# Loads of the next x issued by ScalarE instead of SyncE, layer 1's masked scores ahead of the last turning, its exponentials later in ScalarE's order, in a two-layer graph attention kernel

## The chip, the cores and the metric

The kernel runs on one core of a Trainium2 chip. A core has a matrix engine (TensorE, PE in the profile; its weight loads are PEld), VectorE (DVE), ScalarE (ACT), GpSimd (POOL) and SyncE (SP), which here only issues transfers. Each engine works through its own list in order, and they meet by semaphores. 16 DMA engines serve the transfers of all issuers. The metric is the device time of one execution in microseconds; the time before is a median of three runs.

## The reference

`x` is 128 graphs of 128 nodes with 512 features, `adj` a 128 x 128 matrix of each graph. Two attention layers follow each other:

```python
# layer 0, 8 heads of 64
Q, K, V = x @ W_q + b_q, x @ W_k + b_k, x @ W_v + b_v
scores = einsum('bihd,bjhd->bhij', Q, K) / sqrt(64)
scores = scores + (a[:, :, None] + c[:, None, :] + b_g + log(adj + 1e-9))[:, None]   # a, c: x @ halves of w_g
x = einsum('bhij,bjhd->bihd', softmax(scores), V).reshape(B, N, D) + x
# layer 1, one head of 512
q, k = x @ Wq + bq, x @ Wk + bk
scores = where(adj == 0, -1e18, einsum('bod,bid->boi', q, k) / sqrt(512))
attn = where(adj == 0, 0, softmax(scores))
x = x + einsum('boi,bie->boe', attn, x) @ Wc
out = (x - mean) * rsqrt(var + 1e-5) * gamma + beta
```

## The kernel before

**Tiling.** The graphs are done in 32 groups of four (`GG = 4`, `NG = 32`). A group has 4 x 128 = 512 columns, so x is held turned, as four chunks `d` of 128 features by 512 columns. For precision every large product is three matmuls: each operand is split into a high part (`x_hi`, rounded, on ScalarE, L778) and the rest (`x_lo`, on GpSimd, L1518), and `hi_lo_part` (L244 to L246) multiplies high by high, high by low, low by high.

**Staging.** Iteration `t` of `step` does layer 0's scores and softmax of group `t`, layer 1 of group `u = t - 1`, and the projections of k and q for group `t + 1`. The heads of a group are handled in four pairs `c`: two heads by four graphs are one `probs` tile of 128 x 1024.

**A pair on its way.** TensorE makes the scores (L535). VectorE adds the bias and takes the row extremes (`maxima`, L1120). ScalarE takes the exponentials (`exps`, L828). VectorE inverts the sums (`recips`, L1130), GpSimd multiplies (`probabilities`, L1510), and VectorE turns 32 x 32 blocks into `turned` (`turn`, L1139). Then SyncE stores `turned` to DRAM and fetches it back with the blocks exchanged into `probsT[c]` (`move_probs`), which TensorE uses in `pv` (L548) in the next step. There is one `turned` tile, so the turning of pair `c` waits until the store of pair `c - 1` has landed (`s_pw`). `probs` is one tile too: the next pair's maxima wait for the turning.

**Layer 1 of group u.** `residual0` (L1146) adds pv, bias and x into `xT_land[u % 2]`, where x itself stood. It is split (`x1hi` L835, `x1lo` L1153), turned into rows `x1n` by 16 transposes (`x1_rows`, L1210, which end in `dve_rows`), multiplied by the combined weight (`g_whole`), and scored against itself (`pair_scores`, L570). `row_term` (L1230) makes a term for each row from `x1n`; `masked_scores` (L1252, L1258) adds it to the scores, applies the mask and takes the row extreme (`dve_max1`). ScalarE takes the exponentials (`exp1`, L873), VectorE turns them (`turn_attention`, L1280), SyncE moves them through DRAM (`move_attention`), ScalarE and VectorE split them (`att1T_high`, `att1T_low` L1271), and TensorE multiplies by `y = x1 @ Wc` (`y_whole`, `y_out` L882, `y_low`; then `context`). `residual1`, the statistics, `norm` and GpSimd's scale and shift end the group.

**The next x.** Group `t + 1` lands in the tile in which group `t - 1` lay (`xT_land[(t + 1) % 2]`), so its four loads (`load_x`) wait until the group before last has left it: for `pair_scores` and `x1lo` of each chunk, and for the last of `x1_rows` once. Then `next_x_high` makes `x_hi` on ScalarE and `next_x_low` makes `x_lo` on GpSimd, chunk by chunk, and `project_k(t + 1, 0)` on TensorE waits for each `x_lo` chunk before its three matmuls of that chunk.

**Orders written by hand.** Each engine's list is a function `step`. SyncE's (L387): `load_adj`, pairs 0 and 1 moved, the four loads of x, pair 2 moved, `load_xn(t + 1, 2)`, `move_attention`, `load_xn(t + 1, 3)`, pair 3 moved, `spread_c`, two loads of xn, the stores of the output. ScalarE's (L981) has behind pair 3's exponentials: `log_adj`, `y_out(u, 0)`, `next_x_high` of chunk 0, `exp1(u)`, `next_x_high` of chunks 1 to 3, `y_out(u, 1)`, `att1T_high`. The logarithm and the exponential need different tables, and a table load stands ahead of each. VectorE's, in `layer1_begin`, ends: `recips(t, 3)`, three row terms, `turn(t, 3)`, `masked_scores(u)`; then `step` goes on with a gate of the next x (`next_gate`, L1165), `turn_attention`, `factors1`, `y_low`. TensorE's (L685): pv of group `u`, scores of `t`, `project_v`, `g_whole`, `pair_scores`, `y_whole` 0 to 3, `project_k(t + 1, 0)`, `project_q(t + 1, 0)`, `project_k(t + 1, 1)`, `context` 0 and 1, and the remaining projections.

Of the kernel before, what the change touches and what calls it, by code (L numbers as in the profile page):

```python
# [24 lines left out]
P = 128  # L25
# [4 lines left out]
C = D // P  # L30
GG = 4
NG = GRAPHS // GG
COLS = GG * P
# [16 lines left out]
def gnn_program(nc, xT, x, adj, wq, wk, wv, wqT1, wkT1, wc, bq0, bk0, bv0, wg, bg, bq1, bk1,  # L50
# [9 lines left out]
    with ExitStack() as ctx:  # L60
# [13 lines left out]
        xT_land = [sb(f"xT_land{i}", [P, C, COLS]) for i in range(2)]  # L74
# [110 lines left out]
        def nth(name, t, k=0):  # L185

            return t * PER[name] + k + 1
# [85 lines left out]
        def _(sp):  # L273
            def load_x(t, d):
                sp.dma_start(xT_land[t % 2][:, d, :], xT[t * P:(t + 1) * P, d * COLS:(d + 1) * COLS])\  # L275
                  .then_inc(s_x[d], 16)
# [5 lines left out]
                sp.wait_ge(s["dve_a"], nth("dve_a", t - (g < 2), (g + 2) % 4))  # L282
                sp.dma_start(xn[g % 2][:, :], x[t * COLS + g * P:t * COLS + (g + 1) * P, :]).then_inc(s_xn[g % 2], 16)

            def move_probs(t, c):

                sp.wait_ge(s["dve_t"], nth("dve_t", t, c))
                if t > 0:
                    sp.wait_ge(s["pe_pv"], nth("pe_pv", t - 1, c))
                elif c >= 2:  # L290
                    sp.wait_ge(s_lo["c"], C)
                else:
                    sp.wait_ge(s_lo["v"], C)
                sp.dma_start(turn_dram[c], turned[:, :, :, :].rearrange("p b k s -> p (b k s)"))\
                    .then_inc(s_pw[c], 16)
                sp.wait_ge(s_pw[c], 16 * (t + 1))
                for b in range(P // BLK):
                    sp.dma_start(probsT[c][b * BLK:(b + 1) * BLK, :, :, :].rearrange("r a k s -> r a (k s)"),
                                 turn_dram[c].rearrange("(a r) (b x) -> b r a x", a=P // BLK, b=P // BLK)[b])\
                        .then_inc(s_pt[c], 16)  # L300

            def spread_c(t):

# [83 lines left out]
            def step(t):  # L387
                u = t - 1
                sp.wait_ge(s["dve_mask"], nth("dve_mask", u))
                load_adj(t + 1)  # L390
                for c in range(2):
                    move_probs(t, c)
                for d in range(C):
                    sp.wait_ge(s["pe_sa"], nth("pe_sa", u, d))
                    sp.wait_ge(s["dve_x1"], nth("dve_x1", u, d))
                    if d == 0:
                        sp.wait_ge(s["dve_rows"], nth("dve_rows", u))
                    load_x(t + 1, d)
                move_probs(t, 2)
                load_xn(t + 1, 2)  # L400
                move_attention(u)
                load_xn(t + 1, 3)
                move_probs(t, 3)
                spread_c(t + 1)
                if t + 2 < NG:
                    for g in range(2):
                        load_xn(t + 2, g)
                for g in range(GG):
                    store_rows(u, g)
# [365 lines left out]
        def _(act):  # L775
# [23 lines left out]
            def log_adj(t):  # L799
                if t > 0:  # L800
                    act.wait_ge(s["dve_max"], nth("dve_max", t - 1, 7))
                act.wait_ge(s_adj[t % 2], 16 * (t // 2 + 1))
                nc.scalar.activation(ln_adj[:, :, :], adj_sb[t % 2][:, :, :], ACT.Ln,
                                     bias=eps_c).then_inc(s["act_ln"], 1)
# [90 lines left out]
            def rows_out(t, g):  # L895
                act.wait_ge(s_rows_pe, g + 1)
                nc.scalar.activation(rows_land(t)[:, g, :], rows_bank(g)[:, :], ACT.Copy).then_inc(s_rows_act, 1)

            def next_x_high(t, d):
                if d == 0:  # L900
                    act.wait_ge(s["pe_v"], nth("pe_v", t, GG - 1))
                act.wait_ge(s_x[d], 16 * (t + 2))
                x_hi_chunk((t + 1) % 2, d)
# [55 lines left out]
            def layer1_begin(t):  # L959

                u = t - 1
                for c in range(C):
                    x1hi(u, c)
                exps(t, 0, 0)
                exps(t, 0, 1)
                v_out(t, 0)
                v_out(t, 1)
                exps(t, 1, 0)
                exps(t, 1, 1)
                v_out(t, 2)  # L970
                g_out(u, 0)
                g_out(u, 1)
                exps(t, 2, 0)
                exps(t, 2, 1)
                g_out(u, 2)
                g_out(u, 3)
                v_out(t, 3)
                exps(t, 3, 0)
                exps(t, 3, 1)

            def step(t):  # L981

                u = t - 1
                layer1_begin(t)
                log_adj(t + 1)
                y_out(u, 0)
                next_x_high(t, 0)
                exp1(u)
                for d in range(1, C):
                    next_x_high(t, d)  # L990
                y_out(u, 1)
                att1T_high(u)
                k_out(t + 1, 0)
                q_out(t + 1, 0)
                y_out(u, 2)
                y_out(u, 3)
                k_out(t + 1, 1)
                q_out(t + 1, 1)
                norm(u, 0)
                k_out(t + 1, 2)  # L1000
                norm(u, 1)
                q_out(t + 1, 2)
                norm(u, 2)
                k_out(t + 1, 3)
                norm(u, 3)
                q_out(t + 1, 3)
# [47 lines left out]
        def _(dve):  # L1054
# [77 lines left out]
            def turn(t, c):  # L1132

                dve.wait_ge(s["pool_p"], nth("pool_p", t, 2 * c + 1))
                if c > 0:
                    dve.wait_ge(s_pw[c - 1], 16 * (t + 1))
                elif t > 0:
                    dve.wait_ge(s_pw[C - 1], 16 * t)
                nc.vector.transpose(turned[:, :, :, :],  # L1139
                                    probs[:, :, :].rearrange("p k (b r) -> p b k r", b=P // BLK))\  # L1140
                  .then_inc(s["dve_t"], 1)
# [258 lines left out]
            def layer1_begin(t):  # L1400

                u = t - 1
                for c in range(C):
                    residual0(u, c)
                maxima(t, 0)
                for c in range(C):
                    x1lo(u, c)
                recips(t, 0)
                x1_rows(u, 0, 2)
                turn(t, 0)  # L1410
                maxima(t, 1)
                x1_rows(u, 2, 6)
                recips(t, 1)
                x1_rows(u, 6, 8)
                turn(t, 1)
                maxima(t, 2)
                x1_rows(u, 8, 12)
                recips(t, 2)
                x1_rows(u, 12, 14)
                turn(t, 2)  # L1420
                maxima(t, 3)
                x1_rows(u, 14, 16)
                row_term(u, 0)
                recips(t, 3)
                row_term(u, 1)
                row_term(u, 2)
                row_term(u, 3)
                turn(t, 3)
                masked_scores(u)

            def step(t):

# [20 lines left out]
            def final_step(t):  # L1453

                u = t - 1
                layer1_begin(t)
                turn_attention(u)
                factors1(u)
                y_low(u, 0)
                residual0(t, 0)  # L1460
                residual0(t, 1)
                y_low(u, 1)
                x1lo(t, 0)
                x1lo(t, 1)
                penalties(t)
                residual0(t, 2)
                x1lo(t, 2)
                att1T_low(u)
                residual0(t, 3)
                x1lo(t, 3)  # L1470
                y_low(u, 2)
                y_low(u, 3)
                for g in range(GG):
                    residual1(u, g)
                for g in range(GG):
                    row_term(t, g)
                masked_scores(t, LAST)
                factors1(t)
                residual_last(t, 0)
                residual_last(t, 1)  # L1480
                center(t, 0)
                residual_last(t, 2)
                finish(t, 0)
                center(t, 1)
                residual_last(t, 3)
                dve.wait_ge(s["dve_res"], nth("dve_res", t, 3))
                nc.vector.bn_stats(bnst[:, :], rows_land(t)[:, 3, :]).then_inc(s["dve_bn"], 1)
                carry_wait(s["dve_bn"], nth("dve_bn", t, 0), 2 * C + 3)
                nc.vector.bn_aggr(lnst[:, 3, 0:2], bnst[:, :]).then_inc(s["dve_mean"], 1)
                finish(t, 1)  # L1490
                center(t, 2)
                center(t, 3)
                finish(t, 2)
                finish(t, 3)
# [140 lines left out]
```

## Time and profile before

| | |
|---|---|
| median of three runs | 2360.61 us (2357.82 to 2362.62) |
| profiled execution, its own time | 2356.35 us |
| its span, first to last instruction | 2354.6 us |
| busy | PE 2259.9 us (96%), PEld 1872.5, DVE 1856.3 (79%), ACT 1240.2 (53%), POOL 906.8 (39%) |
| mean granted TensorE clock | 0.989 of full speed |
| DMA | 277.82 MB, 118 GB/s in the mean |

All times are microseconds from the start of the span. Matmuls are pipelined: each is shown longer than the time it adds, so their starts are compared and not their durations. In the list of waits a line names who waited, whose end released it, the total, how often, and the longest. A wait for several semaphores is put down to the one that came last. "SPq" and "ACTq" are the issues of transfers by SyncE and ScalarE. An engine's idle time ahead of an operation stands in brackets behind it; where there is no bracket the engine went straight on.

### The profile page before, as it was taken

How to read it: one execution, taken by the hardware profiler on the slowest of the kernel's cores; microseconds unless marked ns; L12 is line 12 of the kernel's file. 1: busy time of each engine (PE TensorE's matmuls, PEld its weight loads, DVE VectorE, ACT ScalarE, POOL GpSimd, SP SyncE). 2: the span in 40 equal slices, each digit the busy share in tenths (PEclk: the TensorE clock that was granted, in tenths of full speed). 3: DMA queues.
4: the chain of work that ended last, by engine and by line, in shares of the span. 5: the costliest groups of instructions: out<-in, count | busy, mean ns of one | idle time of the engine just before them, and what ended most of it. 6: DMA issues, size and time to landing. Idle time of an engine off the chain costs nothing.

```text
span 2354.6 us, 39731 instructions
## 1 busy us (share of the span) xinstructions
PE 2259.9 (96%) x13256; PEld 1872.5 (80%) x13256; DVE 1856.3 (79%) x5371; ACT 1240.2 (53%) x3492; POOL 906.8 (39%) x1139
## 2 busy tenths in 40 slices
PE   9999999999999999999999999999999999999998
PEld 6877788777887878877788877778777787777886
DVE  6687788777878787887788877877778778778886
ACT  6555555455554445555455545555455554555554
POOL 2144243443443433444424344334343343442443
PEclk9999999999999999999999999999999999999999
DMA  6333333333333343333333343333333333333332
GB/s 220 113 120 123 123 111 104 121 126 121 109 116 116 114 130 118 110 110 118 120 122 114 103 125 126 125 116 110 108 117 126 117 108 117 111 128 121 111 103 71
DMA packets 204061, 277.82 MB, mean 118 GB/s; under 512 B 26064, under 2 KB 128208, under 8 KB 203728
## 3 DMA queue, kind: packets, MB, share of 16 engines
q1 hardware_dynamic: 203568, 274.75, 36.5%
q8 instruction: 105, 1.72, 0.3%
q14 instruction: 100, 0.82, 0.1%
q10 hardware_dynamic: 288, 0.52, 0.1%
HBM read 166.34 MB, written 108.85 MB: 117 GB/s over the span
## 4 chain that ended last, share of the span: by engine, by line
PE 41%; DVE 24%; POOL 12%; issue 10%; DMA 8%; ACT 3%; SPq 2%; DVEq 0%
PE bank L244 11%; PE bank L245 11%; PE bank L246 11%; DVE x1n L1210 8%; POOL probs L1510 8%; DMA turn_dram<-turned 7%; DVE probs L1120 7%; PE bank L548 5%; POOL x_lo L1518 4%; DVE x_lo L1153 3%; ACT att L873 2%; SPq L275 2%; PE bank L535 2%; DVE att L1252 1%; DVE nmax L1120 1%
## 5 line engine op out<-in xcount | busy, mean ns | idle before, releaser
L1510 POOL TENSOR_TENSOR probs<-probs,rcp 128x512 f32<-128x512 f32 x256 | 275.8, 1098 | 792.2 <-DVE rcp L1130 792.0
L828 ACT ACTIVATE probs<-probs,nmax 128x128 f32<-128x128 f32 x1024 | 397.5, 392 | 36.0 <-DVE nmax L1120 36.0
L1210 DVE STREAM_TRANSPOSE x1n<-xT_land 32x512 f32<-32x512 f32 x496 | 348.5, 703 | 9.9
L244 PE MATMUL bank<-x_hi,wk_hi 128*128 128x512 f32 x512 | 215.3, 420 | 82.6 <-POOL x_lo L1518 82.4
L1139 DVE STREAM_TRANSPOSE turned<-probs 128x1024 f32<-128x1024 f32 x128 | 159.4, 1246 | 148.0 <-DMA turn_dram<-turned 85.4
L1518 POOL TENSOR_TENSOR x_lo<-xT_land,x_hi 128x512 fp32r<-128x512 f32 x124 | 165.4, 1356 | 241.0 <-ACT x_hi L778 241.0
L1120 DVE CUSTOM_DVE_ANT_0 probs<-bank,ln_adj 128x128 f32<-128x128 f32 x1024 | 227.1, 287 | 4.1
L244 PEld LDWEIGHTS bank<-x_hi,wk_hi 128*128 128x128 f32 x512 | 98.5, 192 | 137.8 <-POOL x_lo L1518 120.9
L246 PE MATMUL bank<-x_hi,wk_lo 128*128 128x512 f32 x512 | 206.4, 403 | 0.0
L245 PE MATMUL bank<-x_lo,wk_hi 128*128 128x512 f32 x512 | 206.1, 403 | 0.0
L244 PE MATMUL bank<-wc_hi,x_hi 128*128 128x512 f32 x512 | 203.2, 397 | 0.0
L244 PE MATMUL bank<-wv_hi,x_hi 128*128 128x512 f32 x512 | 203.1, 397 | 0.0
L244 PE MATMUL bank<-x_hi,wq_hi 128*128 128x512 f32 x512 | 201.8, 394 | 0.0
L245 PE MATMUL bank<-x_lo,wq_hi 128*128 128x512 f32 x512 | 200.9, 392 | 0.0
L246 PE MATMUL bank<-x_hi,wq_lo 128*128 128x512 f32 x512 | 200.2, 391 | 0.0
L246 PE MATMUL bank<-wv_hi,x_lo 128*128 128x512 f32 x512 | 199.5, 390 | 0.0
L244 PE MATMUL bank<-x_hi,wm_hi 128*128 128x512 f32 x512 | 199.5, 390 | 0.0
L245 PE MATMUL bank<-wc_lo,x_hi 128*128 128x512 f32 x512 | 199.4, 389 | 0.0
L246 PE MATMUL bank<-wc_hi,x_lo 128*128 128x512 f32 x512 | 199.4, 389 | 0.0
L245 PE MATMUL bank<-wv_lo,x_hi 128*128 128x512 f32 x512 | 199.3, 389 | 0.0
L246 PE MATMUL bank<-x_hi,wm_lo 128*128 128x512 f32 x512 | 199.2, 389 | 0.0
L245 PE MATMUL bank<-x_lo,wm_hi 128*128 128x512 f32 x512 | 199.2, 389 | 0.0
(154 smaller groups left out, 5199.9 us busy)
## 6 DMA issues: line engine op xcount, KB each, us to landing
turn_dram<-turned SPq DMA_DIRECT2D x128, 512.0 KB, 2.9
probsT<-turn_dram SPq DMA_DIRECT2D x512, 128.0 KB, 2.7
xT_land<-in_xT SPq DMA_DIRECT2D x126, 256.0 KB, 4.2
xn<-in_x SPq DMA_DIRECT2D x126, 256.0 KB, 3.9
out<-x1n SPq DMA_DIRECT2D x124, 256.0 KB, 2.0
adj_sb<-in_adj SPq DMA_DIRECT2D x32, 256.0 KB, 3.0
c_rows<-c_dram SPq DMA_DIRECT2D x31, 256.0 KB, 4.3
at_dram<-scratch SPq DMA_DIRECT2D x31, 256.0 KB, 2.3
```

The lines of the kernel that those rows point to most:

```text
L244: nc.tensor.matmul(out_ap, st[0], mv[0], start=start, stop=False)
L245: nc.tensor.matmul(out_ap, st[0], mv[1], start=False, stop=False)
L246: return nc.tensor.matmul(out_ap, st[1], mv[0], start=False, stop=stop)
L275: sp.dma_start(xT_land[t % 2][:, d, :], xT[t * P:(t + 1) * P, d * COLS:(d + 1) * COLS])\
L548: mm = nc.tensor.matmul(b[e * HD:(e + 1) * HD, g * P:(g + 1) * P], v_sb[:, g, c * P + e * HD:c * P + (e + 1) * HD], probsT[c][:, :, e * GG ...
L828: op = nc.scalar.activation(probs[:, k, :], probs[:, k, :], ACT.Exp, bias=nmax[:, k:k + 1], scale=-1.0, accum_out=sums[:, k:k + 1])
L1120: op = nc.vector.tensor_tensor_reduce(out=probs[:, k, :], in0=s_banks(c)[h][:, (k % HALF) * P:(k % HALF + 1) * P], in1=ln_adj[:, k % HALF, ...
L1139: nc.vector.transpose(turned[:, :, :, :], probs[:, :, :].rearrange("p k (b r) -> p b k r", b=P // BLK))\
L1153: nc.vector.tensor_tensor(lo[:, c, :], x1_land(t)[:, c, :], hi[:, c, :].bitcast(f32), ALU.subtract).then_inc(s["dve_x1"], 1)
L1210: op = nc.vector.transpose(x1n[b * BLK:(b + 1) * BLK, :, :] .rearrange("p g (c a s) -> p a c g s", c=C, a=P // BLK)[:, a, :, :, :], x1_lan ...
L1510: nc.gpsimd.tensor_tensor(probs[:, half, :], probs[:, half, :], rcp[:, half].unsqueeze(2).to_broadcast([P, HALF, P]), ALU.mult)\
L1518: nc.gpsimd.tensor_tensor(x_lo[:, c, :], xT_land[(t + 1) % 2][:, c, :], x_hi[:, c, :].bitcast(f32), ALU.subtract).then_inc(s["pool_x"], 1)
```

## The change

`load_x` goes from SyncE's list to ScalarE's, with the same waits; the four loads stand there directly behind pair 3's exponentials. `move_probs` is cut into a store and a fetch that are still called one after the other. On ScalarE `next_x_high` of chunk 1 goes ahead of `exp1`. On VectorE `masked_scores(u)` goes ahead of `turn(t, 3)` in every step. In the final step `residual0(t, 0)` goes ahead of `turn_attention(u)`, and `residual0(t, 1)` ahead of `factors1(u)` and `y_low(u, 0)`. The first step keeps its loads of x on SyncE.

```diff
@@ SyncE, step @@
                 for c in range(2):
                     move_probs(t, c)
-                for d in range(C):
-                    sp.wait_ge(s["pe_sa"], nth("pe_sa", u, d))
-                    sp.wait_ge(s["dve_x1"], nth("dve_x1", u, d))
-                    if d == 0:
-                        sp.wait_ge(s["dve_rows"], nth("dve_rows", u))
-                    load_x(t + 1, d)
                 move_probs(t, 2)
@@ ScalarE @@
+            def load_x(t, d):
+                act.wait_ge(s["pe_sa"], nth("pe_sa", t - 2, d))
+                act.wait_ge(s["dve_x1"], nth("dve_x1", t - 2, d))
+                if d == 0:
+                    act.wait_ge(s["dve_rows"], nth("dve_rows", t - 2))
+                act.dma_start(xT_land[t % 2][:, d, :], xT[t * P:(t + 1) * P, d * COLS:(d + 1) * COLS])\
+                   .then_inc(s_x[d], 16)
@@ ScalarE, step @@
                 layer1_begin(t)
+                for d in range(C):
+                    load_x(t + 1, d)
                 log_adj(t + 1)
                 y_out(u, 0)
-                next_x_high(t, 0)
+                for d in range(2):
+                    next_x_high(t, d)
                 exp1(u)
-                for d in range(1, C):
+                for d in range(2, C):
                     next_x_high(t, d)
@@ VectorE, layer1_begin @@
                 row_term(u, 3)
+                masked_scores(u)
                 turn(t, 3)
-                masked_scores(u)
@@ VectorE, final_step @@
                 layer1_begin(t)
+                residual0(t, 0)
                 turn_attention(u)
+                residual0(t, 1)
                 factors1(u)
                 y_low(u, 0)
-                residual0(t, 0)
-                residual0(t, 1)
                 y_low(u, 1)
```

## Rows read from the trace of the kernel before

**Rows 1.** Waits, whole span: waiter <- ended by: us in all, times, longest.

```profile
DVE turned L1139 <- DMA turn_dram<-turned: 85.4, 30, 4.0
PE bank L244 <- POOL x_lo L1518: 82.4, 72, 3.5
```

**Rows 2.** TensorE's timeline, one step: start us, us, engine, line, operation [idle before].

```profile
1029.90 3.71 PE L548 MATMUL bank<-probsT,v_sb 128*64 128x128 f32 x64
...
1059.22 3.73 PE L570 MATMUL bank<-xT_land,k_sb 128*128 128x128 f32 x32
...
1073.69 0.39 PE L244 MATMUL bank<-x_hi,wk_hi 128*128 128x512 f32 x1
...
1079.84 0.39 PE L244 MATMUL bank<-x_hi,wq_hi 128*128 128x512 f32 x1
...
1085.29 0.39 PE L244 MATMUL bank<-y_hi,att1T_hi 128*128 128x512 f32 x1
...
1101.70 3.71 PE L548 MATMUL bank<-probsT,v_sb 128*64 128x128 f32 x64
```

**Rows 3.** Span with mean granted clock; TensorE at first pv, a gap, last pv.

```profile
core 0: 2354.6 us, clock 0.989
...
84.79 0.99 PE L548 MATMUL bank<-probsT,v_sb 128*64 128x128 f32 x14
...
1151.99 0.64 PE L244 MATMUL bank<-x_hi,wk_hi 128*128 128x512 f32 x1
...
2262.40 3.71 PE L548 MATMUL bank<-probsT,v_sb 128*64 128x128 f32 x64
```

**Rows 4.** GpSimd's timeline of the same step, the chunks of x_lo.

```profile
1066.92 1.61 POOL L1518 TENSOR_TENSOR x_lo<-xT_land,x_hi 128x512 fp32r<-128x512 f32 x1 [0.99 <-ACT x_hi L778]
1075.23 3.75 POOL L1518 TENSOR_TENSOR x_lo<-xT_land,x_hi 128x512 fp32r<-128x512 f32 x3 [6.70 <-ACT x_hi L778]
```

**Rows 5.** ScalarE's timeline of the same step, behind pair 3's exponentials.

```profile
1063.41 1.28 ACT L803 ACT_TABLE_LOAD   x1
1064.70 0.72 ACT L803 ACTIVATE ln_adj<-adj_sb,consts 128x512 f32<-128x512 f32 x1
...
1072.98 0.41 ACT L873 ACTIVATE att<-att,stats 128x128 f32<-128x128 f32 x1 [4.83 <-DVE stats L1258]
...
1074.54 1.65 ACT L778 ACTIVATE x_hi<-xT_land 128x512 fp32r<-128x512 f32 x3
```

**Rows 6.** VectorE's timeline of the same step.

```profile
1057.94 1.25 DVE L1139 STREAM_TRANSPOSE turned<-probs 128x1024 f32<-128x1024 f32 x1 [0.64 <-POOL probs L1510]
...
1066.63 0.75 DVE L1230 CUSTOM_DVE_ANT_0 scratch<-x1n,v_b,consts 128x512 f32<-128x512 f32 x1
...
1069.96 1.25 DVE L1139 STREAM_TRANSPOSE turned<-probs 128x1024 f32<-128x1024 f32 x1 [2.57 <-DMA turn_dram<-turned]
1071.13 1.09 DVE L1252 SCALAR_TENSOR_TENSOR att<-bank,r_c,att 128x128 f32<-128x128 f32 x4
...
1081.68 0.69 DVE L1271 TENSOR_TENSOR att1T_lo<-c_rows,att1T_hi 128x512 fp32r<-128x512 f32 x1
```

**Rows 7.** SyncE's timeline, the chain of waits, DMA issues of the whole (median us to landing).

```profile
1062.56 1.79 SPq L275 DMA_DIRECT2D xT_land<-in_xT  x4
...
1064.44 5.43 DMA turn_dram<-turned
...
turn_dram<-turned SPq DMA_DIRECT2D x128, 512.0 KB, 2.9
```

**Rows 8.** ScalarE's issues at the start; x's landings, 200 to 2260 us; a crowded load.

```profile
0.73 0.86 ACTq L786 DMA_DIRECT2D xT_land<-in_xT  x2
...
DMA to landing us min/median/max: 3.0/4.1/6.1
...
probsT<-in_wc SPq DMA_DIRECT2D x4, 256.0 KB, 8.9
```

**Rows 9.** VectorE's timeline, final step: pair 3's turning.

```profile
2299.79 1.24 DVE L1139 STREAM_TRANSPOSE turned<-probs 128x1024 f32<-128x1024 f32 x1
```

More of the change, by code:

```diff
@@ L283, in load_xn, with store_probs @@
                 sp.dma_start(xn[g % 2][:, :], x[t * COLS + g * P:t * COLS + (g + 1) * P, :]).then_inc(s_xn[g % 2], 16)
-            def move_probs(t, c):
+            def store_probs(t, c):
                 sp.wait_ge(s["dve_t"], nth("dve_t", t, c))
@@ L295, in move_probs, with fetch_probs @@
                     .then_inc(s_pw[c], 16)
+            def fetch_probs(t, c):
                 sp.wait_ge(s_pw[c], 16 * (t + 1))
@@ L300, in move_probs @@
                         .then_inc(s_pt[c], 16)
+            def move_probs(t, c):
+                store_probs(t, c)
+                fetch_probs(t, c)
             def spread_c(t):
```

## The prediction

> **What bounds the kernel now.** I read the list of waits first, because busy shares of a kernel in 31 alike steps say little. Two waits of TensorE for the same thing stand out: 82.4 us of idle time, 72 times, ended by `x_lo` on GpSimd; and VectorE idles 85.4 us, 30 times, for the store of `turned` [rows 1]. Then TensorE's timeline of one middle step. It has no gap except in one place: `project_k(t+1, 0)`, whose 12 matmuls start at 1073.69 and whose successor starts at 1079.84, 6.15 us, where the next 24 matmuls take 5.45, so 2.73 for 12 [rows 2]. The rest of the step is rigid: 43.79 from the start of pv to that projection, 5.45 to `context`, 16.41 to the next step's pv [rows 2]. Without the gap a step is 43.79 + 2.73 + 5.45 + 16.41 = 68.38 us. The real mean is (2262.40 - 84.79) / 30 = 72.59 [rows 3]. So **4.21 us of each of 30 steps** is lost at this one place, 126 us in all; part of it is matmuls at the lower of the clock's two levels, 1.2 GHz, since the mean granted clock is 0.989 and such a spell stands right behind the gap in other steps, 0.64 us for a matmul that takes 0.39 [rows 2, 3]. I count them as part of the loss and not beside it.
>
> Who sets the gap? Following back from `x_lo`: its last three chunks start at 1075.23, after three `x_hi` at 1074.54, which stand on ScalarE behind layer 1's exponentials (first at 1072.98, 4.83 idle before it) [rows 4, 5]. Those wait for `masked_scores`, 1071.13, which stands on VectorE behind `turn(t, 3)`, 1069.96, which idled 2.57 for the store of pair 2 [rows 6]. That store was issued only at 1064.44, although pair 2 was turned by 1059.2 (1057.94 + 1.25), because SyncE stood at the loads of x, which wait for `dve_rows`, and issued their four first, from 1062.56. It then shared the DMA engines with 1 MB of x and took 5.43 to land [rows 6, 7]. Every link of this chain is touched.
>
> **The change, part by part**, at the times of that step, TensorE's fixed.
>
> *Loads of x from SyncE to ScalarE.* SyncE loses four issues (1.79 us) and their wait [rows 7]. The store of pair 2 goes at 1059.2 and, at the median 2.9 to landing [rows 7], is down at 1062.1; so `turn(t, 3)` no longer waits for it, but only for GpSimd's products, which end under the row terms. The four fetches of `probsT[2]` follow at about 1062 to 1064, needed only in the next step's pv. Behind them on SyncE stand `load_xn(t+1, 2)` and the move of the attention, which wait for VectorE anyway.
> On ScalarE the loads stand behind pair 3's exponentials, which end at 1063.4 (the table load follows at 1063.41) [rows 5]; the semaphores they wait for have been reached by then (the turned rows were complete when SyncE issued at 1062.56, `pair_scores` starts at 1059.22 and lasts 3.73 [rows 2]). Two issues took 0.86 on ScalarE's queue in the prologue [rows 8], so four take 1.7, as on SyncE: to 1065.1. The engine pays this, where before SyncE did. Queued behind: `log_adj`, `y_out(u, 0)`, `x_hi`. Table load 1.28 and logarithm 0.72 end at 1067.1, `y_out` (as long as an `x_hi`, 0.55) at 1067.7. `ln_adj` is read in the next step, `y_hi[0]` not before `y_low`, after layer 1's factors; neither is late.
>
> *`masked_scores` ahead of `turn(t, 3)`.* The last row term starts at 1066.63 and lasts 0.75 [rows 6]; the masked scores follow at 1067.4. From their start to the first exponential are 1072.98 - 1071.13 = 1.85 us [rows 5, 6]: exponentials possible from 1069.25. The turning moves to 1069.25 to 1070.5, still within 0.7 of its old end. Its store is behind `move_attention` on SyncE, as before, and nothing reads it until the next step.
>
> *Layer 1's exponentials behind `x_hi(1)`.* Two `x_hi` at 0.55 (1.65 for three [rows 5]): 1068.2, 1068.75, if chunks 0 and 1 are down. Issued at 1063.4 and 1063.85 with the median 4.1 to landing [rows 8] they are down at 1067.5 and 1067.95, just in time. Then the second table load, 1.28: 1070.0. So here ScalarE and no longer VectorE sets the exponentials: 1070.0 to 1071.6 (before: 1072.98 to 1074.54), `x_hi(2)` and `(3)` to 1072.7.
> GpSimd: `x_lo(0)` and `(1)` from 1068.3, at most 1.61 each [rows 4], done by 1071.5; `(2)` from 1072.3; at 1.25 (3.75 for three) `(3)` ends at 1074.8, at 1.61 at 1075.5. TensorE needs them, three matmuls or 0.68 apart from 1073.69, at 1075.05 and 1075.73. **Slack 0.2 to 0.9 us; the gap closes.** If x(1) takes the longest landing of the steady part, 6.1 [rows 8], it is down at 1069.95, and 0.55 + 1.28 + 1.56 + 1.1 (two `x_hi`, the second beside `x_lo(2)`) + 0.1 + 2.5 less that overlap of 0.55 puts `x_lo(3)` at 1076.5: 0.8 over. Bounds for the remainder: 0 and 0.8 per step; nothing below 0, as TensorE's other stretches are back to back. I take 0.25, nearer the median row; 30 × 0.25 = 7.5.
>
> *What is late next.* `context` needs `att1T_lo`. It started 8.70 after the first exponential (1081.68) [rows 6]; now the turning and one gate of x stand ahead of `turn_attention`, which makes that 9.0: 1079.0, done 1079.7. TensorE arrives at 1073.69 + 2.73 + 5.45 = 1081.87. Slack 2.2. VectorE's later work is relative to TensorE's `context` and moves with it.
>
> *Final step.* There the store of pair 2 does not wait behind x: the turning follows the row term without idle time [rows 9]. `masked_scores` gains the turning's 1.2, but the move of pair 3 goes 1.9 later and pushes the attention's store behind it, and `residual0(t, 0)` goes ahead of `turn_attention`. I take 0, between -2 and +2. Everything ahead of 84.79 is unchanged.
>
> **Sum.** 84.79 + 30 × 68.38 + (2354.6 - 2262.40 = 92.2) = 2228.4; plus 7.5 = **2235.9** span [rows 3]. The profiled execution lies 1.75 over its span (2356.35), and the median of the runs 4.26 over it: 2235.9 + 6.0 = **2242**. Ends: 2228.4 - 2 + 6 = 2232 and 2228.4 + 24 + 2 + 6 = 2260.
>
> **Rivals.**
> *R1, part of the gap stays.* In ScalarE's order the exponentials now depend on x(1), and the x loads meet the fetches of pair 2 on the same DMA engines instead of its store; each 1 us beyond 1068.2 costs up to 1 us once the slack is used, and the chain to `att1T_lo` moves with it. For it: the store that met x took 5.4 against 2.9. Against: x itself took 3.0 to 6.1 in the store's company [rows 8]. At 1 to 2.5 us per step: 2264 to 2309, middle 2287. The Trainium skill's page "DMA: Bandwidth & Descriptors", section "Issuing engines are not separate DMA queues", speaks for this rival: DMAs of different engines share the same DMA engines, and another issuer saves only issue time. The trace agrees in so far as the store took longer beside x [rows 7].
> *R2, a table load that costs more when its place is on the path.* The one ahead of the logarithm costs 1.28 and nothing behind it [rows 5]; the one ahead of the exponentials lay in idle time. If both cost twice that, `x_lo(3)` ends 2.6 later, at 1077.4, 1.7 over: 2234.4 + 30 × 1.7 = 2285. The same skill's page "ScalarE: Activation LUTs", section "What ACT_TABLE_LOAD costs", states 1.28 plus a drain of 1.38 per switch; the trace shows the 1.28 and not the drain, as the logarithm starts 1.29 after the load.
> *R3, slower.* Same mechanism as R1, but x(1) so late that the exponentials are later than before. From the sum above `x_lo(3)` ends 6.5 after x(1) lands; the mean loss of 4.21 returns when it lands at 1073.4, 9.6 us after its issue. Only the crowded prologue has a load of 8.9 [rows 8]. At 10.6, 1 us later, it gives 2360 + 30 = 2390.
> *R4, the change does not do what it says*, because another wait holds `masked_scores` where it was: `dve_r`, `pe_sa` and the mask are all done by 1067.4, so little speaks for it. 2358.
>
> **Chances.** Forecast (2232 to 2260) 0.78, R1 0.13, R2 0.04, R3 0.03, R4 0.02. To hold 8 in 10 the range takes in the nearer part of R1 and R2: 2232 to 2285. A difference of 0.2%, 5 us, is about what a measurement of this kernel can tell from none. Faster: 0.78 + 0.13 + 0.04 = 0.95; same 0.02; slower 0.03.
>
> **What the changed profile must show.** `project_k(t+1, 0)` to the next projection in under 3.1 us; pv to pv 68.4 to 68.7; the wait of `turned` for its store gone; layer 1's first exponential about 10.8 us after `pair_scores` starts (13.76 before), ended by the table load rather than by VectorE; `x_lo(3)` done before TensorE's last three matmuls of that projection; the granted clock near 1.0. The prediction is wrong if x(1) lands more than 5.5 us after its issue in most steps, if four issues on ScalarE take far over 1.7, or if a new wait appears ahead of `context` or of pv.

## The result, and the profile after

The changed kernel takes **2235.0 us** (2234.8 to 2236.5, four runs) against 2361.6: ratio 0.9466, 95% interval 0.9449 to 0.9482. The prediction was 2242, with 2232 to 2285. The profiled execution has a span of 2234.5 us (predicted 2235.9), and its own time lies 2.0 above that. Of all executions in this document one stands apart, one of the five of late_fetch below, which took 5809.9 us at a granted clock of 1.0; its cause is not known, and no reading rests on it.

TensorE's timeline of a middle step, with its first and last pv and the span. Columns: start, duration, engine, line, operation:

```profile
core 0: 2234.5 us, clock 0.999
...
84.10 1.09 PE L549 MATMUL bank<-probsT,v_sb 128*64 128x128 f32 x16
...
1007.76 3.73 PE L571 MATMUL bank<-xT_land,k_sb 128*128 128x128 f32 x32
...
1022.23 0.39 PE L244 MATMUL bank<-x_hi,wk_hi 128*128 128x512 f32 x1
...
1024.95 0.39 PE L244 MATMUL bank<-x_hi,wq_hi 128*128 128x512 f32 x1
...
1030.39 0.39 PE L244 MATMUL bank<-y_hi,att1T_hi 128*128 128x512 f32 x1
...
2142.41 3.71 PE L549 MATMUL bank<-probsT,v_sb 128*64 128x128 f32 x64
```

These lines answer to [rows 2, 3]. The start of `project_k(t+1, 0)` to the start of `project_q(t+1, 0)` is 1024.95 - 1022.23 = 2.72 us, where it was 6.15: the gap is closed. The next stretch is 5.44 and that up to the projection 14.47, as before. The mean step is (2142.41 - 84.10) / 30 = **68.61 us** (predicted 68.63, before 72.59), and behind the last pv come 92.1 (92.2 before). The granted clock is 0.999.

ScalarE in the same step, behind pair 3's exponentials; `pair_scores` starts at 1007.76:

```profile
1011.12 0.38 ACTq L905 DMA_DIRECT2D xT_land<-in_xT  x1
...
1012.08 0.87 ACTq L905 DMA_DIRECT2D xT_land<-in_xT  x2
1013.04 1.28 ACT L804 ACT_TABLE_LOAD   x1 [1.11 <-issue]
1014.33 0.73 ACT L804 ACTIVATE ln_adj<-adj_sb,consts 128x512 f32<-128x512 f32 x1
...
1015.44 0.62 ACT L779 ACTIVATE x_hi<-xT_land 128x512 fp32r<-128x512 f32 x1
1016.95 0.63 ACT L779 ACTIVATE x_hi<-xT_land 128x512 fp32r<-128x512 f32 x1 [0.89 <-DMA xT_land<-in_xT]
1017.60 1.28 ACT L874 ACT_TABLE_LOAD   x1
1018.90 0.40 ACT L874 ACTIVATE att<-att,stats 128x128 f32<-128x128 f32 x1
...
1020.46 1.14 ACT L779 ACTIVATE x_hi<-xT_land 128x512 fp32r<-128x512 f32 x2
```

This answers to [rows 5]. The four loads go at 1011.12 to 1012.95, the logarithm's table load waits 1.11 us for them, and `x_hi(1)`, which now stands ahead of the exponentials, idles 0.89 for its chunk of x. The exponentials start at 1018.90, 11.1 behind `pair_scores` (13.8 before), directly behind their table load. VectorE and GpSimd:

```profile
1015.96 1.13 DVE L1264 SCALAR_TENSOR_TENSOR att<-bank,r_c,att 128x128 f32<-128x128 f32 x4
...
1017.72 1.23 DVE L1151 STREAM_TRANSPOSE turned<-probs 128x1024 f32<-128x1024 f32 x1
...
1027.54 0.69 DVE L1283 TENSOR_TENSOR att1T_lo<-c_rows,att1T_hi 128x512 fp32r<-128x512 f32 x1 [0.89 <-ACT att1T_hi L893]
...
1021.15 2.55 POOL L1530 TENSOR_TENSOR x_lo<-xT_land,x_hi 128x512 fp32r<-128x512 f32 x2 [2.20 <-ACT x_hi L779]
```

`masked_scores` starts at 1015.96, 8.2 behind `pair_scores` (11.9 before), and the turning goes on without a pause where it idled 2.57 [rows 6]. The last two `x_lo` end at 1023.70, 15.9 behind `pair_scores`; TensorE wants the last at 16.5. Over the whole run, waits and time from issue to landing (the landing line is of x's tile in 190 to 2140 us, min, median, max; the last is all stores of `turned`):

```profile
ACT x_hi L779 <- DMA xT_land<-in_xT: 34.0, 45, 1.4
...
PEld bank L244 <- POOL x_lo L1530: 7.2, 16, 1.2
...
DMA to landing us min/median/max: 2.9/5.8/8.1
...
turn_dram<-turned SPq DMA_DIRECT2D x128, 512.0 KB, 2.6
```

The landings answer to [rows 7, 8]: the store of `turned` fell from a median of 2.9 to 2.6, but **x now takes 5.8 us, where it took 4.1**, and ScalarE waits for it 45 times. In 29 middle steps the last `x_lo` ends 15.3 to 17.0 behind `pair_scores`, 16.27 in the mean, and in 16 places TensorE's weight loads still wait. The matmuls themselves wait for it 1.8 us in all, where they waited 82.4 [rows 1]; the wait of `turned` for its store is gone.

### The profile page after: what moved, and what is told of

Read it like the earlier page. It is cut to its first block, busy times and chain, and to the rows that moved or that the text cites. A ratio compares the mean times of both kernels' runs of the same rounds, so it can differ in the third digit from the quotient of the medians.

```text
span 2234.5 us, 39731 instructions
## 1 busy us (share of the span) xinstructions
PE 2219.4 (99%) x13256; PEld 1863.8 (83%) x13256; DVE 1838.1 (82%) x5371; ACT 1236.9 (55%) x3492; POOL 899.6 (40%) x1139
## 4 chain that ended last, share of the span: by engine, by line
PE 89%; DVE 3%; DMA 2%; ACT 2%; POOL 2%; issue 1%; SPq 0%; DVEq 0%; ACTq 0%
PE bank L244 25%; PE bank L245 24%; PE bank L246 24%; PE bank L549 5%; PE bank L536 5%; PE bank L571 4%; DMA xT_land<-in_xT 1%; POOL probs L1522 1%; DVE x1n L1222 1%; DVE probs L1132 1%; ACT probs L829 1%; PE bank L446 1%; POOL x_lo L1530 1%; ACT att L874 0%; DVE x_lo L1165 0%
## 5 line engine op out<-in xcount | busy, mean ns | idle before, releaser
L1530 POOL TENSOR_TENSOR x_lo<-xT_land,x_hi 128x512 fp32r<-128x512 f32 x124 | 159.4, 1300 | 133.9 <-ACT x_hi L779 133.7
L244 PE MATMUL bank<-x_hi,wk_hi 128*128 128x512 f32 x512 | 201.2, 393 | 1.9 <-POOL x_lo L1530 1.8
L246 PE MATMUL bank<-x_hi,wk_lo 128*128 128x512 f32 x512 | 199.3, 389 | 0.0
L245 PE MATMUL bank<-x_lo,wk_hi 128*128 128x512 f32 x512 | 199.3, 389 | 0.0
L829 ACT ACTIVATION_READ_ACCUMULATOR probs<-probs,nmax 128x1 f32 x1024 | 191.5, 187 | 0.0
```

The costliest lines, as they stand in the source:

```text
L244: nc.tensor.matmul(out_ap, st[0], mv[0], start=start, stop=False)
L245: nc.tensor.matmul(out_ap, st[0], mv[1], start=False, stop=False)
L246: return nc.tensor.matmul(out_ap, st[1], mv[0], start=False, stop=stop)
L829: op = nc.scalar.activation(probs[:, k, :], probs[:, k, :], ACT.Exp, bias=nmax[:, k:k + 1], scale=-1.0, accum_out=sums[:, k:k + 1])
L1530: nc.gpsimd.tensor_tensor(x_lo[:, c, :], xT_land[(t + 1) % 2][:, c, :], x_hi[:, c, :].bitcast(f32), ALU.subtract).then_inc(s["pool_x"], 1)
```

## The experiments

Every kernel was timed beside the kernel before on its own chip. "Step" is the time from the first to the last pv, divided by 30, from its trace; the next two are means over 29 of these steps, all but the first: `project_k(t+1, 0)` to `project_q` (2.72 when nothing waits), and from there to `context` (5.44 when nothing waits). "Exponentials" and "last x_lo" are means over the same 29 steps, behind the start of `pair_scores`; TensorE wants the last `x_lo` at 16.5 (14.47 to the projection, and three times three matmuls of 0.68).

| kernel | median us | ratio to before (95%) | step | project_k | to context | exponentials | last x_lo ends |
|---|---|---|---|---|---|---|---|
| before | 2361.6 | 1 | 72.59 | 6.73 | 5.60 | 14.1 | 20.1 |
| changed | 2235.0 | 0.9466 (0.9449 to 0.9482) | 68.61 | 2.84 | 5.45 | 11.5 | 16.3 |
| p1 | 2256.9 | 0.9559 (0.9541 to 0.9577) | 69.28 | 3.54 | 5.46 | 11.1 | 17.1 |
| p2 | 2261.7 | 0.9580 (0.9562 to 0.9598) | 69.45 | 3.20 | 5.84 | 10.1 | 16.8 |
| p3 | 2329.3 | 0.9869 (0.9845 to 0.9893) | 71.69 | 5.47 | 5.88 | 14.1 | 18.9 |
| p2p3 | 2256.5 | 0.9554 (0.9526 to 0.9582) | 69.46 | 2.74 | 6.23 | 10.2 | 15.5 |
| p1p2 | 2235.6 | 0.9459 (0.9438 to 0.9480) | 68.64 | 2.86 | 5.44 | 10.3 | 16.4 |
| turn_late | 2233.7 | 0.9469 (0.9454 to 0.9483) | 68.53 | 2.72 | 5.49 | 10.2 | 15.0 |
| sp_between | 2232.5 | 0.9445 (0.9427 to 0.9463) | 68.49 | 2.75 | 5.44 | 10.2 | 15.0 |
| late_fetch | 2230.6 | 0.9438 (0.9420 to 0.9456) | 68.40 | 2.72 | 5.44 | 10.2 | 15.0 |
| dose_y | 2263.0 | 0.9577 (0.9559 to 0.9595) | 69.49 | 3.77 | 5.49 | 12.6 | 17.4 |
| dose_far | 2329.4 | 0.9873 (0.9857 to 0.9890) | 71.72 | (below) | 5.46 | 10.1 | 19.6 |

The theory (A): the gap came from the chain late store of pair 2, turning of pair 3, masked scores, exponentials, `x_hi`, `x_lo`; any cut of it closes the gap. The rival (B): another issuer for x is what counts.

### One part at a time

**p1**, only the loads moved:

```diff
@@ SyncE, step @@
-                for d in range(C):
...
-                    load_x(t + 1, d)
@@ ScalarE, step @@
                 layer1_begin(t)
+                for d in range(C):
+                    load_x(t + 1, d)
                 log_adj(t + 1)
```

> The loads of the next x on ScalarE behind pair 3's exponentials, and nothing else of the change. Theory A (the gap of TensorE comes from the chain store of pair 2, turning of pair 3, masked scores, exponentials, x_hi, x_lo, and any cut of this chain closes it): the turning starts 8.2 us after pair_scores starts (10.5 to 12 before), the exponentials at 11.1 as in the final step of before, three x_hi to 14.3, x_lo(3) at 17.1 against 16.5 when TensorE wants it: 0.7 us of the 4.2 stay in each step, time 2252 (2240 to 2265). Theory B (what matters is only that the loads have another issuer): the whole gain, 2235.

Measured 2256.9. ScalarE and GpSimd in the step whose `pair_scores` starts at 1153.71:

```profile
1162.07 1.28 ACT L867 ACT_TABLE_LOAD   x1
1164.79 0.40 ACT L867 ACTIVATE att<-att,stats 128x128 f32<-128x128 f32 x1 [1.44 <-DVE stats L1262]
...
1166.35 1.66 ACT L772 ACTIVATE x_hi<-xT_land 128x512 fp32r<-128x512 f32 x3
...
1167.04 3.79 POOL L1522 TENSOR_TENSOR x_lo<-xT_land,x_hi 128x512 fp32r<-128x512 f32 x3 [3.63 <-ACT x_hi L772]
```

The exponentials start at 11.08 and end `x_hi` at 14.3, as expected; the three `x_lo` behind them take 3.79 and end at 17.1, 0.65 too late. p1 gives 104.5 of the 126 us, and what is left is GpSimd's three chunks behind the exponentials. B's 2235 is refuted.

**p2**, only the order on VectorE:

```diff
+                masked_scores(u)
                 turn(t, 3)
-                masked_scores(u)
```

> Only the masked scores ahead of the turning of pair 3; the loads of x stay on SyncE ahead of pair 2's store. Theory A: the store still lands late and the turning still waits for it, but nobody on the path waits for the turning any more; the exponentials start 10.1 us after pair_scores, x_lo(3) ends at 16.1, just in time: 2235 (2230 to 2245), although no load has moved. Theory B: most of the loss stays, above 2300.

Measured 2261.7: 100 us of gain although no load has moved, so B is out, but 27 above what A gave and outside its range. The waits of the whole run, and GpSimd in the step whose `pair_scores` starts at 951.31:

```profile
PE bank L244 <- DVE att1T_lo L1271: 9.4, 14, 2.1
...
PE bank L244 <- POOL x_lo L1518: 7.2, 19, 1.2
...
963.63 4.71 POOL L1518 TENSOR_TENSOR x_lo<-xT_land,x_hi 128x512 fp32r<-128x512 f32 x3 [3.02 <-ACT x_hi L778]
```

The waits for `x_lo` fell from 82.4 to 7.2, and a new one has come, at `context`, for `att1T_lo`: A had forgotten who else stands behind the late turning. That is about half of the miss. The other half is still `x_lo`: the exponentials start at 10.1 as expected, but the last `x_lo` ends at 16.8 and not at 16.1, since the three `x_lo` behind them take 4.71 here and 3.79 in p1, and `project_k` loses 0.48 a step. Where the longer time comes from is told under p2p3.

**p3**, only `x_hi` of chunk 1 ahead of the exponentials:

```diff
-                next_x_high(t, 0)
+                for d in range(2):
+                    next_x_high(t, d)
                 exp1(u)
-                for d in range(1, C):
+                for d in range(2, C):
                     next_x_high(t, d)
```

> Only x_hi of chunk 1 ahead of layer 1's exponentials. Theory A: the exponentials stay late (13.7), but only two x_hi and two x_lo stand behind them, so x_lo(3) ends at 18.4 in place of 19.8 or more: a loss of 1.9 to 2.5 per step stays, 2300 (2285 to 2325). Theory B: no change, 2360.

Measured 2329.3, just above the range. `x_lo(3)` ends at 18.9 and not at 18.4, because the exponentials start at 14.1 and not at 13.7; that is 2.4 too late. The 29 steps lose 3.2 in the mean. The 0.8 beyond are in the section on the hardware.

**p2p3**, the edits of p2 and p3 together, no load moved:

> Masked scores ahead of the turning and x_hi of chunk 1 ahead of the exponentials, the loads of x left on SyncE. x is issued at the same time as with the change but is not behind the fetches of pair 2. Theory A: exponentials at 10.1, x_lo(3) at 15.3, more slack than the full change has: no stall left in any step, 2231 (2228 to 2236), at least as fast as the full change at 2235. Theory B: above 2300.

Measured 2256.5 (2248.6 to 2261.1, a wider spread than the other changed kernels have; the trace is of the slowest), not 2231. `project_k` loses nothing any more (2.74), but the way to `context` is 6.23 in place of 5.44 and that from `context` to the next pv 16.62 in place of 16.41. Waits, then VectorE, GpSimd, SyncE and TensorE in the step whose `pair_scores` starts at 1156.29:

```profile
DVE turned L1140 <- DMA turn_dram<-turned: 32.7, 30, 2.8
...
DVE ln_adj L1105 <- DMA c_rows<-c_dram: 28.0, 26, 6.4
PE bank L244 <- DVE att1T_lo L1272: 20.4, 17, 3.0
...
1167.47 1.25 DVE L1140 STREAM_TRANSPOSE turned<-probs 128x1024 f32<-128x1024 f32 x1 [1.16 <-DMA turn_dram<-turned]
1168.64 1.80 DVE L1166 CUSTOM_DVE_ANT_0 scratch<-xn,wg_b,consts 128x512 f32<-128x512 f32 x1
...
1170.38 1.77 DVE L1169 CUSTOM_DVE_ANT_0 xn<-xn,wg_b 128x512 f32<-128x512 f32 x1
...
1172.26 0.71 DVE L1281 STREAM_TRANSPOSE scratch<-att 128x512 f32<-128x512 f32 x1
...
1175.63 0.75 DVE L1166 CUSTOM_DVE_ANT_0 scratch<-xn,wg_b,consts 128x512 f32<-128x512 f32 x1 [1.20 <-DMA at_dram<-scratch]
...
1176.30 0.69 DVE L1169 CUSTOM_DVE_ANT_0 xn<-xn,wg_b 128x512 f32<-128x512 f32 x1
...
1179.91 0.69 DVE L1272 TENSOR_TENSOR att1T_lo<-c_rows,att1T_hi 128x512 fp32r<-128x512 f32 x1 [1.39 <-ACT att1T_hi L892]
...
1168.61 2.99 POOL L1519 TENSOR_TENSOR x_lo<-xT_land,x_hi 128x512 fp32r<-128x512 f32 x2 [1.78 <-ACT x_hi L778]
...
1161.48 0.38 SPq L294 DMA_DIRECT2D turn_dram<-turned  x1
1167.40 1.75 SPq L298 DMA_DIRECT2D probsT<-turn_dram  x4
...
1173.00 0.34 SPq L318 DMA_DIRECT2D at_dram<-scratch  x1
...
1180.65 0.50 PE L244 MATMUL bank<-y_hi,att1T_hi 128*128 128x512 f32 x1 [1.58 <-DVE att1T_lo L1272]
```

The store of pair 2 still goes at 1161.48, behind x, and is down at 1167.4. The turning waits for it (1167.47), the gate and `turn_attention` stand behind the turning (1172.26, 16.0 behind `pair_scores`), the attention goes to DRAM at 1173.0, and `att1T_lo` starts at 1179.91, 23.6 behind. TensorE arrives 22.6 behind and idles 1.58. The late store thus had **two ways** to TensorE, and the second had been hidden as long as the first was longer. VectorE waits for `c_rows` as well (`ln_adj`, 26 times), but late_fetch below, the fastest kernel, has that wait 31 times, 54.2 us in all, so it is no cause.

**The wait for the store is only half of what makes the attention late.** The two operations of the gate behind the turning take 1.80 and 1.77 us here, beside `x_lo` on GpSimd, and 0.75 and 0.69 a little later, when GpSimd is idle. Over the whole trace of p2p3 the second of them takes 1.63 in the 29 places where it meets GpSimd and 0.69 in the 97 others; `x_lo` takes 1.67 beside it, and 1.30 in the changed kernel, where the two never meet. `turn_attention` starts 14.97 behind `pair_scores` in the mean, in sp_between (below) 12.60. Of these 2.4 us 1.2 are the later turning and 1.2 the longer gate. p2 has the same meeting in 30 places, and that is where its last `x_lo` lost 0.7.

Which order holds the attention, VectorE's or SyncE's (rival D)? **turn_late** is p2p3 with the turning behind `turn_attention`:

```diff
                 masked_scores(u)
-                turn(t, 3)
@@ VectorE, step @@
                 next_gate(t + 1, 0)
                 turn_attention(u)
+                turn(t, 3)
                 factors1(u)
```

> As p2p3 (loads of x on SyncE ahead of pair 2's store, masked scores ahead of the turning, x_hi of chunk 1 ahead of the exponentials), and the turning of pair 3 behind turn_attention as well. p2p3 lost 0.9 us per step at context, for att1T_lo. Theory A: that is because the turning, which waits for the late store, stands on VectorE ahead of the gate and turn_attention; with it behind them att1T_lo starts at about 20.5 in place of 21 to 23, and the loss is gone: 2234 (2230 to 2240). Rival D: it is SyncE, which waits for the same store and fetches pair 2 before it can store the attention, and the loss stays: 2250 or more.

Measured 2233.7, the wait nearly gone:

```profile
PE bank L244 <- DVE att1T_lo L1272: 1.8, 3, 0.8
```

So it was VectorE's order; `att1T_lo` starts 21.0 behind `pair_scores` in the mean (22.5 in p2p3). This order takes away both the wait and the meeting of gate and `x_lo` (one place is left), so how much of p2p3's loss each alone would give is not shown. D costs 1.1 us, hidden in the slack: the attention's store goes at 13.4, in sp_between at 13.3, but takes 3.5 to land in place of 2.5, beside the late fetches of pair 2, and `att1T_lo` starts at 21.0 in place of 19.9. With this a kernel that never moves a load of x is as fast as the change.

**p1p2**, the change without chunk 1 ahead of the exponentials and with the old final step. Against the change:

```diff
@@ ScalarE, step @@
-                for d in range(2):
-                    next_x_high(t, d)
+                next_x_high(t, 0)
                 exp1(u)
-                for d in range(2, C):
+                for d in range(1, C):
                     next_x_high(t, d)
@@ VectorE, final_step @@
-                residual0(t, 0)
                 turn_attention(u)
-                residual0(t, 1)
                 factors1(u)
                 y_low(u, 0)
+                residual0(t, 0)
+                residual0(t, 1)
```

> Loads on ScalarE and masked scores ahead of the turning, but x_hi of chunk 1 behind the exponentials, as before the change, and the final step as before. Theory A: the exponentials start at 10.1 to 10.8, three x_hi end near 13.5, and three x_lo at 16.4 to 16.9 against the 16.5 at which TensorE wants the last: 0.1 to 0.5 us per step, 2239 (2233 to 2248). Rival: the place of chunk 1 is what closes the gap, 2255 or more.

Measured 2235.6; the change has 2235.0, and 2235.5 in the run below. **The third part of the change is worth nothing beside the other two**: the exponentials start 1.2 earlier without it (10.3 against 11.5), since they do not wait for x(1), and one more `x_hi` and `x_lo` stand behind them. Both end at 16.3 to 16.4. The final step's new order is worth nothing either: from the last pv to the end p1p2 takes 92.3 and the change 92.1, in its second trace 91.6.

### Who slows whom

**sp_between**: the change, with the loads taken from ScalarE and put back on SyncE, between the store and the fetches of pair 2.

```diff
+                store_probs(t, 2)
+                for d in range(C):
...
+                    load_x(t + 1, d)
+                fetch_probs(t, 2)
-                move_probs(t, 2)
```

> The changed kernel, but the four loads of x back on SyncE, between the store and the fetches of pair 2. Theory A (what counts is that the store of pair 2 does not stand behind the loads; the issuer does not matter): x is issued at 3.35 us after pair_scores as with ScalarE, ahead of the fetches, so it lands in 4 us as in the kernel before and not in 5.8; the exponentials start at 10.1, and no step loses anything to x_lo: 2231 (2228 to 2236), no slower than the changed kernel (2235). Theory C (a second issuing queue is what makes it fast): slower than the change by 5 us or more.

Measured 2232.5. Time from issue to landing of x:

```profile
DMA to landing us min/median/max: 2.9/3.9/7.0
```

**late_fetch**: the change, with the fetches of pair 2 later on SyncE. The loads stay on ScalarE.

```diff
-                move_probs(t, 2)
+                store_probs(t, 2)
                 load_xn(t + 1, 2)
                 move_attention(u)
                 load_xn(t + 1, 3)
+                fetch_probs(t, 2)
```

> The changed kernel, but SyncE fetches pair 2 back only behind move_attention and load_xn(t+1, 3); the loads of x then have no other transfer beside them. Theory A (x's landing rose from 4.1 to 5.8 us because the fetches of pair 2 run beside it): median landing back to about 4, exponentials at 10.1 to 10.5 in place of 11.5, the waits for x_lo gone: 2232 (2228 to 2240). Theory C' (ScalarE's queue is itself slower): landing stays at 5.8, 2235.

Measured 2230.6, and x:

```profile
DMA to landing us min/median/max: 2.7/3.8/5.6
```

In both the landing is back at 3.8 to 3.9: it was the fetches of pair 2 that made x slow, and ScalarE's queue is as fast as SyncE's. late_fetch has no wait for `x_lo` left and sp_between four of TensorE's weight loads (2.3 us), and both run at 68.4 to 68.5 per step, within 0.02 to 0.11 of the 68.38 without any wait. C, a second queue as the cause, is refuted by sp_between. The difference of 4 us to the change was measured again on one chip:

> The changed kernel once more, on the same chip as the next run, to compare the two. All theories: 2235.

> The changed kernel with the fetches of pair 2 behind move_attention and load_xn(t+1, 3), once more beside the changed kernel. Theory A: 4 us faster than the changed kernel, 2231; if the difference seen before was that of two chips: the same as the changed kernel.

2235.5 (2234.9 to 2235.8) and 2231.0 (2230.8 to 2233.6), ratios to before 0.9477 and 0.9460: the two runs' ranges lie apart by 1.3 us, the intervals of the ratios overlap. late_fetch is the fastest kernel of this study.

### How late may x be?

**dose_y**: the loads behind `log_adj` and `y_out(u, 0)`.

```diff
-                for d in range(C):
-                    load_x(t + 1, d)
                 log_adj(t + 1)
                 y_out(u, 0)
+                for d in range(C):
+                    load_x(t + 1, d)
```

> The changed kernel with the four loads of x behind the logarithm and y_out(u, 0) in ScalarE's order, issued about 3.1 us later. Theory A with the arithmetic of the prediction's rival R1 (x_lo(3) ends 6.5 us after x(1) lands, slack under 1 us): x(1) lands at 11.0 to 12.7 in place of 9.6, x_lo(3) at 17.6 to 19.2, a loss of 1.1 to 2.7 us per step: 2290 (2268 to 2316), still faster than before. If late loads were as harmless as idle time on ScalarE suggests: 2235 to 2245.

Measured 2263.0, just below the range. The last `x_lo` ends at 17.4, not 17.6 to 19.2, because x, issued at 6.6 in place of 3.35, now comes after the fetches and lands in a median of 3.7. The loss of 1.05 per step at `project_k` fits 17.4 - 16.5 = 0.9.

**dose_far**: the loads and all `x_hi` behind the exponentials.

```diff
-                for d in range(C):
-                    load_x(t + 1, d)
                 log_adj(t + 1)
                 y_out(u, 0)
-                for d in range(2):
-                    next_x_high(t, d)
                 exp1(u)
-                for d in range(2, C):
+                for d in range(C):
+                    load_x(t + 1, d)
+                for d in range(C):
                     next_x_high(t, d)
```

> The changed kernel with the four loads of x, and x_hi of all chunks, behind layer 1's exponentials in ScalarE's order. ScalarE's queue runs ahead of its engine, so they go when the exponentials' wait is over, at 10.1 us after pair_scores: 6.7 later than with the change. x(0) lands at 13.7, x_lo(0) ends at 15.8, and the chain of four x_lo at 1.27 ends at 19.6 against 16.5: 3.1 to 3.4 us lost per step, 2326 (2310 to 2350). If the loads were issued only at the end of the exponentials: 1.6 more, 2370, no faster than the kernel before.

Measured 2329.4. The first exponential and the first load, then TensorE's wait and the clock:

```profile
1200.51 0.40 ACT L874 ACTIVATE att<-att,stats 128x128 f32<-128x128 f32 x1 [1.69 <-DVE stats L1268]
1200.61 0.33 ACTq L905 DMA_DIRECT2D xT_land<-in_xT  x1
...
PE bank L244 <- POOL x_lo L1528: 64.0, 118, 2.0
...
core 0: 2327.5 us, clock 0.998
```

The load is issued at 1200.61, 0.1 after the first of the exponentials begins and 1.5 before they end: ScalarE's queue does run ahead of its engine. The last `x_lo` ends at 19.6, as expected. (The stretch is not in the table because the wait for the first chunk lies ahead of it.)

## Why the prediction was right, point by point

**The bound.** The whole gain was read from one gap. 68.38 for a step without it was right: late_fetch comes to 68.40. That TensorE's other stretches are back to back held in the changed kernel. It did not hold in p2 and p2p3, nor in three places of turn_late, where the cover of `att1T_lo` was gone, nor in dose_far, where even the first `x_lo` is late; what before and p3 show above 5.44 on the way to `context` comes with no wait there, but with the lower clock.

**The chain.** Right at each link, by p1 (turning at 8.1 in place of 11.1, exponentials at 11.1) and p2 (exponentials at 10.1). The prediction treated the change as one chain, and did not say that the first two parts each suffice to break it: p1 gives 105 us, p2 100, both together 128 (p1p2, each against the kernel before on its own chip). They are not terms of a sum.

**Issue of the loads on ScalarE.** Priced at 1.7 from 1063.4, the end of pair 3's exponentials. It starts 3.35 behind `pair_scores`, when `dve_rows` comes, and not at 4.2: the issues run under the last exponentials, and the engine loses 1.11 and not 1.7. Wrong, to the safe side.

**Landing of x.** Taken as 4.1, the median of before; measured 5.8. This is the term that failed: R1 named its mechanism, the fetches of pair 2 in the same DMA engines, and the trace of before had x beside the store and not beside fetches. x(1) took over 5.5 us in 20 of 29 steps (median 5.75; in the second trace of the kernel 14 of 29, median 5.50; before 3.8). So the sign that the prediction gave for being wrong, over 5.5 in most steps, did appear. x(1) was down at 8.5 to 10.2 behind `pair_scores`, in 25 steps at 9.1 or later, and not at 8.7, and the exponentials started at 11.5, not 10.8. The time came out near the forecast all the same, because a second error went the other way: the loads were issued 0.8 us earlier than the sum had them. That is luck. With it the slack of 0.2 to 0.9 just held: in the mean 0.2. With the issue at the exponentials' end, as I had it, the same arithmetic gives a mean end of 17.1, a loss in most steps; that was argued and not run.

**The remainder.** Predicted 0.25 a step, measured 68.61 - 68.38 = 0.23. That is luck in part: 4.1 us of the 7 fall in the first of the 30 steps (72.48), where the sum had none, and the other 29 lose 0.10 each. In the second trace of the same kernel the first step is 70.83, so the first step varies from one execution to the next.

**What is late next.** `context` was given a slack of 2.2: `att1T_lo` starts 20.4 behind `pair_scores` in the mean and is wanted done at 22.6, so 1.5. It had the right place: it is where p2 and p2p3 lost.

**Table load (R2).** Both cost 1.28 and nothing behind: 1013.04 to 1014.33, and 1017.60 to 1018.90, the second on the path. The drain that the Trainium skill's page "ScalarE: Activation LUTs", section "What ACT_TABLE_LOAD costs", adds does not appear here.

**Slower (R3).** dose_far is the nearest to it: with x issued 6.8 us later than in the change the kernel is still 1.3% faster than before. The point at which it turns was not reached.

**Span to median.** The change's runs lie 2.0 over their spans, and its median is only 0.5 above the span of the profiled one, where I had added 6.0 from before, whose profiled execution was faster than all of its timed runs. That is 5.5 of the 7 us by which 2242 is off; 1.4 are the span.

## What to carry to other kernels

In an in-order list the wait of an instruction is paid by everything behind it, so look for a store that has been ready for long and stands behind a load that is not; either the load or the order of the consumer may be moved, and one of them is usually enough. When a gap has been traced to one late event, list every engine that waits for that event before pricing a partial cure: p2p3 closed the gap that was visible and kept a loss of 1.1 us per step (69.46 against 68.40, in the slowest of its four executions) on the way that had been hidden. Look there too for what the moved work now meets: half of that delay was VectorE beside GpSimd, each slowing the other. A load moved to another queue still shares the DMA engines, so price its landing by the transfers that will run beside it, and put those without a hurry, like the fetches of pair 2, behind it.

## What the runs showed of the hardware

*A transfer's landing depends on its company, not on its issuer.* 256 KB loads of x, four in a row: 4.1 us beside a store, 5.8 beside four fetches (ScalarE's queue), 3.9 ahead of them (SyncE's), 3.8 without them (ScalarE's). The Trainium skill's page "DMA: Bandwidth & Descriptors", section "Issuing engines are not separate DMA queues", states that transfers run on the same 16 DMA engines and interleave, whichever engine issued them. These runs agree: ScalarE's loads slowed beside SyncE's fetches, 5.8 against 3.8. What another issuer did save here was the waiting in SyncE's list, not bandwidth.

*ScalarE issues DMAs while it still works through earlier activations* (dose_far), and the next activation waits until they are issued, 0.48 apart (1011.12 to 1012.95 for four).

*VectorE's gate and GpSimd's `x_lo` slow each other where they meet.* `xn<-xn,wg_b` takes 0.69 alone and 1.63 in the mean beside GpSimd (p2p3), `x_lo` 1.67 beside it and 1.30 in the changed kernel. Not every operation of VectorE does this: in late_fetch `x_lo` takes 1.31 in the mean beside the turning of pair 3.

*The same loss cost clock in one kernel and hardly any in another.* p3 and dose_far take the same time. The waits for `x_lo` and the clock of p3, then TensorE behind one of its waits, and the stretch from 1137 to 1139 (its last three numbers: granted clock, share and GB/s of the DMA engines):

```profile
PE bank L244 <- POOL x_lo L1519: 59.5, 57, 3.4
...
core 0: 2327.4 us, clock 0.988
...
1135.77 0.50 PE L244 MATMUL bank<-x_hi,wk_hi 128*128 128x512 f32 x1 [2.44 <-POOL x_lo L1519]
...
1137.61 0.63 PE L245 MATMUL bank<-x_lo,wk_hi 128*128 128x512 f32 x1
...
1137.00:1139.00 2.00, 1.98 (x5) 1.61 (x6) 1.65 (x5) 0.00 (x0) 0.00 (x0) 0.50 0.23 66
```

p3 has fewer and longer waits (57, up to 3.4 us) and a granted clock of 0.988; dose_far has more and shorter ones (118, up to 2.0) and 0.998. In p3 the last `x_lo` is 2.4 too late and the 29 steps lose 3.2 each; in dose_far 3.1 and 3.2. The difference is matmuls at the lower level, 1.2 GHz, behind the long waits, 0.63 us each where they take 0.39: the clock is at that level for 53.9 us in all in p3, and for 8.4 in dose_far. By the same reckoning 0.6 of the 4.1 us of the kernel before were clock (20.1 - 16.5 = 3.6), an estimate of 18 us in all; its trace has 53.6 us at the lower level, which at half speed can cost 27 at most. The change gave this back with the gap. No run varied the length of a wait alone, so from where a wait costs clock stays open.
